# Directed layers: a fused subtract-and-maximum for the low half of the left values, and one-tensor forms for denominator and epsilon

## The chip, the cores and the metric

The kernel runs on one core of one Trainium2 chip. A core has TensorE (PE, with its weight loads, PEld), VectorE (DVE), ScalarE (ACT), GpSimd (POOL) and SyncE (SP, which issues the transfers). Each engine runs its own queue of instructions in order; engines are tied together by semaphores alone. The metric is the device time of one execution in microseconds.

## The reference, cut to what matters

There are 64 graphs of 128 nodes with 384 features, and four layers, each of the form x = x + layer(relu(layernorm(x)), adj). Layers 0 and 3 are attention layers. Layer 1 is a directed layer, and layer 2 is two such layers one behind the other. The changed code computes the directed ones:

```python
u = einsum('bld,bmd->blm', h, h) / sqrt(d)
p = softmax(u, axis=-1)
delta = p * adjacency
attn = delta / (sum(delta, axis=2, keepdims=True) + 1e-10)
h_left  = h @ W_left.T + b_left     # likewise h_self, h_right
ctx = einsum(where(j > i, attn, 0), h_left) + diag_a * h_self + einsum(where(j < i, attn, 0), h_right)
o = (ctx - mean) / sqrt(var + 1e-12) * gamma + beta
return relu(o)
```

The kernel does not divide by the row sum. It carries the context unnormalised and adds 1e-12 times the square of the (scaled) denominator to the variance, which gives the same `o`. That is what `den`, `scaled_den` and `eps` are for.

## The kernel before

All matrix products are done in float16 with every operand split into a high and a low half (`hi` = the value rounded to float16, `lo` = the value minus `hi`), three products for each (`three_products`, lines 138 to 141: L139, L140 and L141 in the profile).

`directed` (from line 916) runs once for L1, with 64 tasks, one for each graph, and once for L2, with 128 tasks, two for each graph ("first" and "second"). In L2 first and second tasks of neighbouring graphs alternate. Each engine has a function `step`, called once per task, that lists its work for this task and for the neighbours: `n_.has(0)` is the task itself, `-1` and `-2` are earlier tasks whose tail is done here, `1` and `2` later ones.

One task: `turn_h` transposes h, `turned_hi` (ScalarE) and `turned_lo` (VectorE, L1137, tile `L_hT_lo`) split it. `similarity` gives u, from which `row_max` (L1142) and the exponent are made. `mask` (L1150) multiplies with the adjacency and sums into `tsum`; `diagonal` (L1155) picks the diagonal. Both are `tensor_tensor_reduce`, which the profile shows as CUSTOM_DVE_ANT_0 followed by DVE_READ_ACCUMULATOR2_ANT. `biased` (L1190) makes `left` and `right` from PSUM. `context_var_eps` (L1211, L1212) serves the task before. `denominator` (L1162), `part_sides` (L1180) and `scaled_denominator` (L1168) follow, then `right`, `left_lo` (L1185), `scaled_eps` (L1173), the addition to x of the task two before (`add_to_x`, L1217, only where that one is not a "first"), statistics of the graph two ahead (`stats`, L1123, only in half of L2's tasks) and `turned_lo` of the next task. ScalarE makes the high halves: left (L1065), sides (`sides_hi`, L1069), then `norm_ctx` (L1081, tile `L_o`), then right (L1065). GpSimd does `ctx_norm` (L993, L995), `sides_lo` (L999), `right_lo` (L1004), `gain` (L1009), `offset` (L1019) and, for a graph two ahead, `norm` (L985, L987).

TensorE, per task: similarity, the left and right projections, the transpose for the next task, the self projection, then the six context matmuls: three for left (needs `left_lo`, `sides_lo`), two with the right values' high half (L1325, L1326), and L1328, which waits for `right_lo`. Next comes the similarity of the next task, which waits for `turned_lo`.

The order of VectorE's queue inside one task is written out by hand:

```python
denominator(n_)
part_sides(n_)
scaled_denominator(n_)
biased(n_, d["r_psum"], d["r_sum"], d["r_lo"], right, r_bank, tables[n_.kind()][3])
left_lo(n_)
scaled_eps(n_)
```

Of the kernel before, what the change touches and what calls it, by code (L numbers as in the profile page):

```python
# [23 lines left out]
ALU = mybir.AluOpType  # L24
# [4 lines left out]
P = 128  # L29
# [7 lines left out]
EPS_LN = 1e-12  # L37
MASKED = -9e15
LOWEST = -3.4e38
LIFT = 2.0 ** 12  # L40
# [89 lines left out]
def wait(eng, sem, value):  # L130

    if isinstance(value, int) and value <= 0:
        return
    eng.wait_ge(sem, value)
# [9 lines left out]
def build(nc, ins, out):  # L144
    with ExitStack() as ctx:
        def sb(stack, name, shape, dt=F32):
            return stack.enter_context(nc.sbuf_tensor(name, shape, dt))
# [756 lines left out]
        d = {}  # L904
# [8 lines left out]
        def directed(tag, phase, graph_base, weights, extras, bias_rows, tables, next_weights):  # L913
# [5 lines left out]
            with ExitStack() as s:  # L919
# [3 lines left out]
                leftv = [sb(s, f"{tag}_left_{a}", [P, D], F16) for a in ("hi", "lo")]  # L923
                rightv = [sb(s, f"{tag}_right_{a}", [P, D], F16) for a in ("hi", "lo")]
                left = sb(s, f"{tag}_left", [P, D])
# [20 lines left out]
                nmax = sb(s, f"{tag}_nmax", [P, 1])  # L946
                zsum = sb(s, f"{tag}_zsum", [P, 1])
                tsum = sb(s, f"{tag}_tsum", [P, 1])
                diag = sb(s, f"{tag}_diag", [P, 1])
                den = sb(s, f"{tag}_den", [P, 1])  # L950
                scaled_den = sb(s, f"{tag}_scaled_den", [P, 1])
                eps = sb(s, f"{tag}_eps", [P, 1])
# [10 lines left out]
                with nc.Block() as block:  # L963
# [155 lines left out]
                    def _(dve):  # L1119
# [39 lines left out]


                        def denominator(n_):
                            dve.scalar_tensor_tensor(out=den[:, :], in0=zsum[:, :], scalar=1e-10 * LIFT, in1=tsum[:, :],  # L1162
                                                     op0=ALU.mult, op1=ALU.add).then_inc(d["den_ready"], 1)

                        def scaled_denominator(n_):
                            wait(dve, d["den_ready"], n_.done())
# [3 lines left out]

                        def scaled_eps(n_):
                            wait(dve, d["scaled_den_ready"], n_.done())
                            dve.scalar_tensor_tensor(out=eps[:, :], in0=scaled_den[:, :], scalar=EPS_LN, in1=scaled_den[:, :],  # L1173
                                                     op0=ALU.mult, op1=ALU.mult).then_inc(d["eps_ready"], 1)

                        def part_sides(n_):

# [4 lines left out]

                        def left_lo(n_):
                            wait(dve, d["l_hi"], n_.done())
                            dve.tensor_tensor(leftv[1][:, :], left[:, :], leftv[0][:, :], ALU.subtract).then_inc(d["l_lo"], 1)  # L1185

                        def biased(n_, psum_sem, sum_sem, lo_sem, full, bank, bias):
                            wait(dve, psum_sem, n_.done())
# [31 lines left out]
                        def step(n_):  # L1220
# [27 lines left out]
                            if n_.has(0):  # L1248
# [6 lines that stand above are left out]
# [114 lines left out]
        for tag, phase, base, weights, next_weights, kinds in (  # L1369
                ("L1", Phase(0, first=4, last=6, after=2), 0, W1, W2, ("only",)),  # L1370
                ("L2", TwoLayerPhase(G, first=3, last=3, after=2), G, W2, W3, ("first", "second"))):
            with ExitStack() as s:
                w_hi, w_lo = (sb(s, f"{tag}_w_{a}", [P, 3 * len(kinds), C, D], F16) for a in ("hi", "lo"))
                bias_rows = sb(s, f"{tag}_bias_rows", [P, len(kinds), D], F16)
                kept_rows = sb(s, f"{tag}_gain_offset_biases", [P, len(kinds), 4, D])

                rows_of = [(n, [5 * n + 1], n) for n in range(len(kinds))]

                def bias_rows_high(act, weights=weights, rows=bias_rows, rows_of=rows_of):
                    weights.bias_rows_high(act, rows, rows_of)  # L1380

                def bias_rows_low(dve, weights=weights, rows=bias_rows, rows_of=rows_of):
                    weights.bias_rows_low(dve, rows, rows_of)

                def keep_rows(pool, weights=weights, number=len(kinds), kept=kept_rows):

                    pool.wait_ge(w_scaled, weights.n_prepared + 1)
                    for n in range(number):
                        pool.tensor_copy(kept[:, n, 0:2], raw_bias[:, 5 * n + 3:5 * n + 5]).then_inc(w_kept_by_pool, 1)
                        for m, b in ((2, 0), (3, 2)):  # L1390
                            pool.tensor_scalar(kept[:, n, m], raw_bias[:, 5 * n + b], scale[:, n:n + 1], None,
                                               ALU.mult).then_inc(w_kept_by_pool, 1)

                weights.begin(w_hi, w_lo, len(kinds), 3 * len(kinds))
                extras = {"act": bias_rows_high, "dve_before": bias_rows_low, "pool": keep_rows}
                directed(tag, phase, base, weights, extras, bias_rows,
                         {kind: [kept_rows[:, n, m] for m in range(4)] for n, kind in enumerate(kinds)}, next_weights)
# [63 lines left out]
```

## Time and profile before

| | |
|---|---|
| median of 3 runs | 2719.62 us (2717.78 to 2720.9) |
| profiled execution | 2719.79 us, span 2718.1 us, mean granted clock 0.981 |
| TensorE busy | 2501.8 us (92%) |
| VectorE busy | 2323.3 us (85%) |
| ScalarE busy | 1815.9 us (67%) |
| GpSimd busy | 1439.5 us (53%) |
| `L_left_lo` (L1185), 192 times | 173.4 us, mean 903 ns |
| `L_den` (L1162), 192 times | 28.4 us, mean 148 ns |
| `L_eps` (L1173), 192 times | 38.9 us, mean 203 ns |

In the profile, a row of the timeline gives the start in us from the span's start, the duration in us, engine, line, operation, tile written and tiles read with their shapes, and in brackets the idle time before it with what ended it. L1 runs from about 655 to 1103 us, L2 from about 1155 to 2005 us. The durations of neighbouring instructions of one engine overlap a little, since the next one starts before the last has drained: what an instruction costs its queue is the distance from its start to the next one's start.

### The profile page before, as it was taken

The page shows a single profiled execution, that of the slowest core. Times are in us where ns is not written, and L with a number is a line of the kernel's source. Part 1 is how long each engine was busy: PE and PEld are TensorE (multiplying, and loading weights), DVE is VectorE, ACT ScalarE, POOL GpSimd, SP SyncE. Part 2 cuts the span into 40 slices and gives each one's busy share as a digit, 9 for nine tenths or more (in the row PEclk, how much of TensorE's full clock was granted, in tenths as well). Part 3 has the DMA queues.
Part 4 walks back from the last instruction along what each step waited for, and adds up shares of the span by engine and source line. Part 5 has one row for each costly group of instructions (what it writes and reads, how often), then busy time and mean ns, then how long its engine had stood idle before and what let it go on. Part 6 is the DMA issues. An engine that isn't in the chain of part 4 may idle for free. (4 is left out here: it accounts for less than half of the span.)

```text
span 2718.1 us, 80319 instructions
## 1 busy us (share of the span) xinstructions
PE 2501.8 (92%) x27969; PEld 1884.9 (69%) x27969; DVE 2323.3 (85%) x9515; ACT 1815.9 (67%) x4409; POOL 1439.5 (53%) x2016
## 2 busy tenths in 40 slices
PE   5999999986999999599999999999969999999998
PEld 4888888884666665466666666666648888888886
DVE  5787878776999999688888888888869999999997
ACT  5888888874556555455566566655638777777775
POOL 2232323223777777467777777777734444444443
PEclk9999999997999999899999999999979999999999
DMA  3111111102000000100000000000000000000000
GB/s 106 29 34 30 33 30 34 29 19 88 10 11 11 11 10 11 45 11 11 11 12 11 11 11 12 11 11 11 12 6 23 28 27 26 29 26 29 26 30 24
DMA packets 74340, 64.67 MB, mean 24 GB/s; under 512 B 7888, under 2 KB 73936, under 8 KB 73936
## 3 DMA queue, kind: packets, MB, share of 16 engines
q1 hardware_dynamic: 73936, 59.54, 7.2%
q8 instruction: 223, 3.65, 0.6%
q14 instruction: 181, 1.48, 0.2%
HBM read 46.92 MB, written 12.58 MB: 22 GB/s over the span
## 5 line engine op out<-in xcount | busy, mean ns | idle before, releaser
L139 PE MATMUL bank<-L_w_hi,L_hT_hi 128*128 128x384 f16 x2112 | 692.3, 328 | 0.0
L140 PE MATMUL bank<-L_w_lo,L_hT_hi 128*128 128x384 f16 x2112 | 692.1, 328 | 0.0
L141 PE MATMUL bank<-L_w_hi,L_hT_lo 128*128 128x384 f16 x2112 | 691.5, 327 | 0.0
L540 ACT ACTIVATE raw_weights<-L_minus_scores,L_minus_max 128x128 f32<-128x128 f32 x1536 | 474.8, 389 | 69.7 <-DVE L_minus_max L655 69.7
L139 PE MATMUL bank<-L_hT_hi,L_w_hi 128*128 128x128 f16 x2304 | 412.6, 220 | 1.3 <-issue 0.8
L140 PE MATMUL bank<-L_hT_lo,L_w_hi 128*128 128x128 f16 x2304 | 412.6, 220 | 0.0
L141 PE MATMUL bank<-L_hT_hi,L_w_lo 128*128 128x128 f16 x2304 | 412.3, 220 | 0.0
L655 DVE CUSTOM_DVE_ANT_0 L_minus_scores<-bank,L_minus_score_bias 128x128 f32<-128x128 f32 x1536 | 348.7, 285 | 10.6 <-issue 6.4
L682 DVE TENSOR_TENSOR L_pT_lo<-bank,L_pT_hi 128x512 f16<-128x512 f32 x384 | 241.1, 683 | 118.4 <-ACT L_pT_hi L562 118.3
L141 PEld LDWEIGHTS bank<-L_w_hi,L_hT_lo 128*128 128x128 f16 x2112 | 207.4, 98 | 138.2 <-issue 2.6
L1059 ACT ACTIVATE L_e<-bank,L_nmax 128x128 f32<-128x128 f32 x192 | 70.5, 367 | 342.6 <-DVE L_nmax L1144 342.6
L473 POOL TENSOR_TENSOR L_ln_scale_bias<-L_var_eps,minus_half 128x1 f32<-128x1 f32 x128 | 70.2, 549 | 402.1 <-DVE L_var_eps L621 401.1
L140 PEld LDWEIGHTS bank<-L_w_lo,L_hT_hi 128*128 128x128 f16 x2112 | 207.4, 98 | 108.5 <-issue 2.0
L139 PEld LDWEIGHTS bank<-L_w_hi,L_hT_hi 128*128 128x128 f16 x2112 | 208.0, 99 | 98.8 <-issue 2.0
L481 POOL TENSOR_TENSOR L_xsum<-L_attended,L_bias_v 128x384 f32<-128x384 f32 x64 | 64.1, 1001 | 383.7 <-DVE L_attended L703 383.7
L1004 POOL TENSOR_TENSOR L_right_lo<-L_right,L_right_hi 128x384 f16<-128x384 f32 x192 | 212.2, 1105 | 89.9 <-ACT L_right_hi L1065 87.2
L562 ACT ACTIVATE L_pT_hi<-bank 128x512 f16<-128x512 f32 x384 | 200.6, 596 | 45.4 <-PE bank L831 45.4
L139 PEld LDWEIGHTS bank<-L_hT_hi,L_w_hi 128*128 128x128 f16 x2304 | 226.7, 98 | 2.3 <-issue 2.2
L140 PEld LDWEIGHTS bank<-L_hT_lo,L_w_hi 128*128 128x128 f16 x2304 | 226.8, 98 | 0.7
L141 PEld LDWEIGHTS bank<-L_hT_hi,L_w_lo 128*128 128x128 f16 x2304 | 226.8, 98 | 0.0
L993 POOL TENSOR_TENSOR L_cln_scale_bias<-L_cvar_eps,minus_half 128x1 f32<-128x1 f32 x192 | 105.7, 550 | 219.1 <-DVE L_cvar_eps L1212 219.1
L1019 POOL TENSOR_TENSOR L_ob<-L_og,L_gain_offset_biases 128x384 f32<-128x384 f32 x192 | 191.3, 997 | 15.1
(165 smaller groups left out, 7514.4 us busy)
## 6 DMA issues: line engine op xcount, KB each, us to landing
adj_tile<-in_adj SPq DMA_DIRECT2D x320, 64.0 KB, 1.8
x<-in_x SPq DMA_DIRECT2D x64, 192.0 KB, 2.5
out<-L_result SPq DMA_DIRECT2D x64, 192.0 KB, 1.9
raw_weights<-in_L_gnn_Wq SPq DMA_DIRECT2D x2, 576.0 KB, 4.1
raw_weights<-in_L_gnn_Wk SPq DMA_DIRECT2D x2, 576.0 KB, 5.5
raw_weights<-in_L_gnn_Wv SPq DMA_DIRECT2D x2, 576.0 KB, 5.2
raw_weights<-in_L_gnn_Wl SPq DMA_DIRECT2D x2, 576.0 KB, 5.9
raw_weights<-in_L_gnn_Ws SPq DMA_DIRECT2D x2, 576.0 KB, 5.5
```

The costliest lines, as they stand in the source:

```text
L139: pe.matmul(out, stat[0], move[0], start=first, stop=False)
L140: pe.matmul(out, stat[0], move[1], start=False, stop=False)
L141: return pe.matmul(out, stat[1], move[0], start=False, stop=last)
L473: pool.tensor_tensor(ln[:, 0:1], ve[:, 0:1], minus_half[:, :], ALU.pow).then_inc(rstd_ready, 1)
L540: last = act.activation(probs[:, n_.slot(k), i, :], scores[:, i, :], ACT.Exp, bias=nmax[:, n_.slot(k), i:i + 1], scale=-1.0)
L562: act.activation(pT[0][:, HC * c:HC * c + HC, :], pT_banks[c][:, :].rearrange("p (h q) -> p h q", h=HC), ACT.Copy).then_inc(pT_hi[c], 1)
L655: last = dve.tensor_tensor_reduce(scores[:, i, :], s_banks[j][:, c128(c)], bias[:, n_.slot(), :], 1.0, -LOWEST, ALU.add, ALU.min, nmax[:, ...
L682: dve.tensor_tensor(pT[1][:, hs, :], pT_banks[c][:, :].rearrange("p (h q) -> p h q", h=HC), pT[0][:, hs, :], ALU.subtract).then_inc(pT_lo[ ...
L993: pool.tensor_tensor(cln[:, 0:1], cve[:, 0:1], minus_half[:, :], ALU.pow).then_inc(d["crstd_ready"], 1)
L1004: pool.tensor_tensor(rightv[1][:, :], right[:, :], rightv[0][:, :], ALU.subtract).then_inc(d["r_lo"], 1)
L1019: pool.tensor_tensor(ob[:, :], og[:, :], tables[n_.kind(k)][1], ALU.add).then_inc(d["tail_ready"], 1)
L1059: act.activation(e[:, :], u_bank[:, 0:P], ACT.Exp, bias=nmax[:, 0:1], scale=scalev, accum_out=zsum[:, :]).then_inc(d["p_ready"], 1)
```

## The change

`left_lo` becomes a `tensor_tensor_reduce`: it writes the same difference and also reduces it by maximum into a new column `lmax`, which nothing reads. `denominator` and `scaled_eps` were `scalar_tensor_tensor` with two tensors of one column and a constant; they become `tensor_scalar` with one tensor of one column, a constant, and the other column as per-partition scalar operand. Values and order of all queues stay.

```diff
+                lmax = sb(s, f"{tag}_left_low_max", [P, 1])
...
                         def denominator(n_):
-                            dve.scalar_tensor_tensor(out=den[:, :], in0=zsum[:, :], scalar=1e-10 * LIFT, in1=tsum[:, :],
-                                                     op0=ALU.mult, op1=ALU.add).then_inc(d["den_ready"], 1)
+                            dve.tensor_scalar(den[:, :], zsum[:, :], 1e-10 * LIFT, tsum[:, 0:1], ALU.mult,
+                                              ALU.add).then_inc(d["den_ready"], 1)
...
                         def scaled_eps(n_):
                             wait(dve, d["scaled_den_ready"], n_.done())
-                            dve.scalar_tensor_tensor(out=eps[:, :], in0=scaled_den[:, :], scalar=EPS_LN, in1=scaled_den[:, :],
-                                                     op0=ALU.mult, op1=ALU.mult).then_inc(d["eps_ready"], 1)
+                            dve.tensor_scalar(eps[:, :], scaled_den[:, :], EPS_LN, scaled_den[:, 0:1], ALU.mult,
+                                              ALU.mult).then_inc(d["eps_ready"], 1)
...
                         def left_lo(n_):
                             wait(dve, d["l_hi"], n_.done())
-                            dve.tensor_tensor(leftv[1][:, :], left[:, :], leftv[0][:, :], ALU.subtract).then_inc(d["l_lo"], 1)
+                            dve.tensor_tensor_reduce(leftv[1][:, :], left[:, :], leftv[0][:, :], 1.0, LOWEST, ALU.subtract, ALU.max,
+                                                     lmax[:, :]).then_inc(d["l_lo"], 1)
```

## Rows read from the trace of the kernel before

**Rows 1.** Windows: stretch (us), length, busy us (instructions) of PE, PEld, DVE, ACT, POOL, PEclk, DMA
```profile
690.00:1060.00 370.00, 362.66 (x2504) 225.90 (x2502) 342.79 (x1280) 217.93 (x479) 281.42 (x427) 1.00 0.04 11
1250.00:1950.00 700.00, 694.88 (x4964) 447.62 (x4963) 611.92 (x2273) 419.50 (x950) 508.11 (x738) 1.00 0.04 11
```
**Rows 2.** Waits in L1, 690 to 1060 us: who waited for whom, us, times, longest
```profile
PEld bank L1328 <- POOL L_right_lo L1004: 22.7, 53, 0.6
PEld bank L139 <- DVE L_hT_lo L1137: 17.8, 53, 0.7
```
**Rows 3.** Timeline, TensorE, L1: last context matmul and first of the next similarity
```profile
834.78 0.34 PE L1328 MATMUL bank<-L_right_lo,L_sides_hi 128*128 128x384 f16 x1
835.21 0.23 PE L139 MATMUL bank<-L_hT_hi 128*128 128x128 f16 x1
```
**Rows 4.** Timeline, VectorE, the same L1 task and the next
```profile
832.50 0.91 DVE L1185 TENSOR_TENSOR L_left_lo<-L_left,L_left_hi 128x384 f16<-128x384 f32 x1
833.34 0.15 DVE L1173 SCALAR_TENSOR_TENSOR L_eps<-L_scaled_den 128x1 f32<-128x1 f32 x1
833.41 0.55 DVE L1217 SCALAR_TENSOR_TENSOR x<-L_ob,x 128x384 f32<-128x384 f32 x1
...
834.62 0.52 DVE L1137 TENSOR_TENSOR L_hT_lo<-bank,L_hT_hi 128x384 f16<-128x384 f32 x1
...
835.92 0.29 DVE L1142 TENSOR_REDUCE L_nraw<-bank 128x1 f32<-128x128 f32 x1
```
**Rows 5.** Timeline, GpSimd, the same L1 task
```profile
832.33 0.67 POOL L999 TENSOR_TENSOR L_sides_lo<-L_sides,L_sides_hi 128x256 f16<-128x256 f32 x1
833.53 1.20 POOL L1004 TENSOR_TENSOR L_right_lo<-L_right,L_right_hi 128x384 f16<-128x384 f32 x1 [0.53 <-ACT L_right_hi L1065]
```
**Rows 6.** Timeline, L1: GpSimd's L987 and VectorE's custom instruction of `diagonal`
```profile
844.28 0.19 POOL L987 TENSOR_TENSOR L_ln_scale_bias<-L_var_eps,L_ln_scale_bias 128x1 f32<-128x1 f32 x1
844.30 0.31 DVE L1155 CUSTOM_DVE_ANT_0 L_junk<-L_e_masked,identity 128x128 f32<-128x128 f32 x1
844.54 0.08 DVE L1155 DVE_READ_ACCUMULATOR2_ANT L_diag<- 128x1 f32 x1
```
**Rows 7.** Timeline, VectorE, L1: small instructions in a row
```profile
838.08 0.20 DVE L1211 TENSOR_SCALAR L_cvar_eps<-L_cmean_var,L_eps 128x1 f32<-128x1 f32 x1
838.20 0.14 DVE L1212 TENSOR_SCALAR L_cvar_eps<-L_cmean_var 128x1 f32<-128x1 f32 x1
838.26 0.14 DVE L1162 SCALAR_TENSOR_TENSOR L_den<-L_zsum,L_tsum 128x1 f32<-128x1 f32 x1
838.32 0.41 DVE L1180 TENSOR_TENSOR L_sides<-bank,ight_of_left_of_diagonal 128x256 f32<-128x256 f32 x1
```
**Rows 8.** Timeline: `sides_hi` in L1; `part_sides` and `sides_hi` in an L2 task with x
```profile
838.77 0.42 ACT L1069 ACTIVATE L_sides_hi<-L_sides 128x256 f16<-128x256 f32 x1
...
1412.66 0.42 DVE L1180 TENSOR_TENSOR L_sides<-bank,ight_of_left_of_diagonal 128x256 f32<-128x256 f32 x1
1413.17 0.40 ACT L1069 ACTIVATE L_sides_hi<-L_sides 128x256 f16<-128x256 f32 x1
```
**Rows 9.** Timeline, L2 task with an x: addition to x and `right_lo`
```profile
1414.73 0.55 DVE L1217 SCALAR_TENSOR_TENSOR x<-L_ob,x 128x384 f32<-128x384 f32 x1
1414.80 1.25 POOL L1004 TENSOR_TENSOR L_right_lo<-L_right,L_right_hi 128x384 f16<-128x384 f32 x1 [0.48 <-ACT L_right_hi L1065]
```
**Rows 10.** Timeline, L2 task without an x: L1328, next similarity, row maximum
```profile
1422.58 0.33 PE L1328 MATMUL bank<-L_right_lo,L_sides_hi 128*128 128x384 f16 x1
1422.78 0.23 PE L139 MATMUL bank<-L_hT_hi 128*128 128x128 f16 x1
1423.51 0.28 DVE L1142 TENSOR_REDUCE L_nraw<-bank 128x1 f32<-128x128 f32 x1
```
**Rows 11.** Timeline, L1: `left_lo` and `sides_lo` starting together
```profile
915.82 0.55 DVE L1185 TENSOR_TENSOR L_left_lo<-L_left,L_left_hi 128x384 f16<-128x384 f32 x1
915.82 1.08 POOL L999 TENSOR_TENSOR L_sides_lo<-L_sides,L_sides_hi 128x256 f16<-128x256 f32 x1 [0.20 <-ACT L_sides_hi L1069]
```

## Prediction

> **What bounds the kernel now.** I read the page first: TensorE is the busiest engine, VectorE the second, and only the two directed stretches hold the changed lines. The windows of the two directed stretches come next [rows 1]: TensorE is busy 362.66 of 370 us in the first (layer L1) and 694.88 of 700 in the second (L2), always at a granted clock of 1.00, its 2.4 GHz level. So little is left to take from it, but whatever delays it is paid. The waits say where it still stops in L1 [rows 2]: 53 times for GpSimd's `right_lo`, 53 times for VectorE's `turned_lo` (tile `L_hT_lo`). A wait that comes 53 times in 370 us means one task in about 7.0 us. The timelines of one task show both. `right_lo` ends at 833.53 + 1.20 = 834.73 and the last context matmul follows at 834.78 [rows 3, 5]; `L_hT_lo` ends at 834.62 + 0.52 = 835.14 and the next similarity starts at 835.21 [rows 3, 4].
>
> Both stops hang on one thing: the two-input reads of VectorE and GpSimd keep each other out. `left_lo` takes 0.91 us for 384 elements, and ends (833.41) 0.41 after `sides_lo` ends (833.00) [rows 4, 5]: it waited for GpSimd, then streamed. Where it starts together with `sides_lo`, it takes 0.55 and `sides_lo` 1.08 instead [rows 11]. One sits still until the other is done, and at a tie VectorE goes first. Then the race repeats: the addition to x starts at 833.41, `right_lo` at 833.53, 0.12 later, loses, and takes 1.20 [rows 4, 5]. Of that 0.29 is blocked time (x streams to 833.41 + 0.41), so 0.91 is its own.
>
> **`left_lo` as tensor_tensor_reduce.** The question is whether the new form keeps clear of GpSimd. The trace answers with the custom instruction of `diagonal`, which has two SBUF inputs too. GpSimd's little L987 starts at 844.28 for 0.19; the custom instruction starts at 844.30 and ends at 844.61, 0.14 after L987's end [rows 6]. 0.14 is the time of 128 elements at the rate at which `left_lo` does 384 in 0.41, so it was released and then streamed, as `left_lo` does. It holds and is held like the old form. The fused form removes no wait, then: it starts at the same place, is released by the same `sides_lo`, and streams at one element at the same rate. What it adds is a read of the accumulator: this starts 0.07 before the custom instruction's end and lasts 0.08 [rows 6], hence between nothing and 0.08. I take nothing, since the read begins where the next instruction of the old form begins, 0.07 before the end [rows 4, 6], and lies almost wholly under the instruction itself. Nobody reads the maximum.
>
> The Trainium skill (Vector Engine (DVE) Microarchitecture Reference, Points that are easy to get wrong) says that a two-input instruction with an accumulator runs at half rate when both sources are SBUF and not bf16. The trace speaks against it: 128 elements in 0.31 including the 0.17 that it stood behind L987. By the page 384 elements would cost some 0.40 more per task; that is a rival below.
>
> **`denominator` and `scaled_eps`.** Both change from two tensors and a constant to one tensor, a constant and a per-partition column. The old form lets the next instruction start after 0.06 to 0.07 (`denominator` 838.26, `part_sides` 838.32; `scaled_eps` 833.34, x 833.41) [rows 4, 7]. The form with a column takes 0.20, and the next instruction starts 0.12 after it (L1211 to L1212), against 0.06 for L1212 without one [rows 7]. So +0.06 for `denominator` and +0.05 for `scaled_eps`; the bounds are 0 (all hidden) and those. `scaled_eps` also stops contending with GpSimd, worth nothing where `left_lo` ends after `sides_lo`.
>
> Where they lie in L1: `denominator` stands ahead of `part_sides`. ScalarE's `sides_hi` starts at 838.77, 0.04 after `part_sides` ends (838.32 + 0.41) [rows 7, 8], so it moves by 0.06, and `sides_lo` and the release of `left_lo` with it. `right_lo` does not move: it follows ScalarE's `norm_ctx` and `right_hi`, which hang on `context_var_eps` ahead of `denominator`. `scaled_eps` is directly between `left_lo` and x. Together the addition to x starts 0.11 later; `right_lo`, blocked until x has streamed, ends 0.11 later; the statistics and `L_hT_lo` are in the same queue behind x and end 0.11 later too. Both stops of TensorE grow together. The next row maximum follows the similarity's start by 0.71 (835.21 to 835.92) [rows 3, 4], and from it the whole next task hangs, so the period grows by the full 0.11. 62 of 64 tasks carry an x: 62 x 0.11 = 6.8 us.
>
> In L2 tasks alternate. In those with an x (A), `sides_hi` starts at 1413.17, 0.09 after `part_sides` ended (1412.66 + 0.42), not 0.04 [rows 8]: ScalarE was busy with the left half. This cover of 0.05 hides `denominator`; without it A would pay 0.06 more. `scaled_eps` is paid: x and with it the blocked `right_lo` (1.25, started 0.07 after x) [rows 9] end 0.05 later, and TensorE waits for that. In those without an x (B) TensorE waits only for `L_hT_lo`: similarity starts 0.20 after the last context matmul (1422.58 to 1422.78), and the row maximum 0.93 after it, now set by the context's addition [rows 10]. I take `sides_hi` there as uncovered, as in L1. `L_hT_lo` then comes 0.11 later, similarity at 0.31, the row maximum at 0.31 + 0.71 = 1.02 instead of 0.93: +0.09. 62 pairs x (0.05 + 0.09) = 8.7 us.
>
> Sum: 6.8 + 8.7 = 15.5 us on the profiled run's 2719.8 (span 2718.1), which is 0.2 above the median: **2735 us**.
>
> **Rivals.** *The race for the port is lost* (slower still). x now starts only 0.01 ahead of `right_lo` in L1 (0.12 - 0.11) and 0.02 in A (0.07 - 0.05) [rows 4, 5, 9]. At a tie VectorE won [rows 11]; 0.02 behind, in `diagonal`, it lost [rows 6]. If x is behind by that, `right_lo` runs its 0.91 alone, to 1.20 + 0.91 = 2.11 after `sides_lo`'s old start, x streams after it and ends at 2.11 + 0.41 = 2.52 instead of 1.63 (833.41 + 0.55 - 832.33). `L_hT_lo` and the period grow by 0.89 in place of 0.11: 62 x 0.89 = 55 us. In A the bounds are 0 and 0.89; `L_hT_lo` is not what TensorE waits for there, so it has slack first, and I take 0.4: 25 us, with B's 5.6. All lost: about 2805. Only A's lost: 6.8 + 25 + 5.6, about 2757.
>
> *The fused instruction does not hold the port* (faster). For it speaks only that rows 6 show small sizes; against it that its end follows L987's end. Then it takes 0.55, x starts 0.61 after `left_lo`'s start (833.11, not 833.41), `right_lo` runs unblocked, and L1 gains 0.30 a task, 19 us. In A at most the blocked 0.34 goes; with 0.28, 17 us. About 2684 us. It decides from the point where `left_lo` is no longer released by `sides_lo`.
>
> *Nothing is seen*: the column forms hidden behind semaphores, as `right` and the matmuls have their own release: 2720.
>
> *Half rate of the fused instruction*: 0.40 on 186 tasks at least, 74 us: 2794, and the race would be lost as well.
>
> **How the numbers follow.** The forecast gets 0.68, with 2726 (only `scaled_eps` paid) to 2746 (the accumulator's read paid in part) as its own range. The lost race gets 0.14, half of it in a part of the tasks only; nothing seen 0.11; the free port 0.05; half rate 0.02. The range 2721 to 2765 takes in the forecast, half of "nothing seen" and the race lost in A alone or now and then. A measurement of this kernel can tell about 0.2% (5.4 us) from no change. Slower by more than that: 0.68 + 0.14 + 0.02 = 0.84; within 0.11; faster 0.05.
>
> **What would show it.** `left_lo`'s fused instruction still at 0.9 to 0.97 us; `denominator` and `scaled_eps` at 0.20; x at 0.55 and starting just before `right_lo`, which takes about 1.31 in L1 and 1.30 in A; L1's period up by 0.11; TensorE's waits for both larger. x at over 1 us and `right_lo` at 0.91 is the lost race. `left_lo` at 0.55 beside a `sides_lo` of 0.67 is the free port. The step I trust least is the 0.01 to 0.02 that is left of the lead.

## The result and the profile after

| | before | changed |
|---|---|---|
| median | 2720.26 us (4 runs) | 2736.26 us (4 runs, 2734.47 to 2739.69) |
| ratio | | 1.0062, 95% interval 1.0044 to 1.0079 |
| span of the profiled execution | 2718.1 us | 2736.3 us |
| L1, second task to last / L2, third task to last | 435.5 / 836.5 us | 440.7 / 846.3 us |
| median period, L1 task / L2 pair | 6.931 / 13.231 us | 7.037 / 13.397 us |

On another chip, with five runs, the changed kernel took 2737.77 us (ratio 1.0066, 1.0053 to 1.0078). The periods here and below are distances from one `right_lo` matmul of TensorE to the next, in the trace.

The three changed instructions in the changed kernel (engine, line, operation, tile, count: shortest/median/longest in ns). One line was added far above, so they stand one line lower.

```profile
L1186 DVE CUSTOM_DVE_ANT_0 L_left_lo<-L_left,L_left_hi x192: 545/958/1060, 660.4 to 2015.3; 128x384 f16<-128x384 f32 x192
L1186 DVE DVE_READ_ACCUMULATOR2_ANT L_left_low_max<- x192: 75/77/86, 661.0 to 2016.2; 128x1 f32 x192
L1163 DVE TENSOR_SCALAR L_den<-L_zsum,L_tsum x192: 196/204/206, 658.2 to 2014.1; 128x1 f32<-128x1 f32 x192
L1174 DVE TENSOR_SCALAR L_eps<-L_scaled_den x192: 202/203/211, 661.0 to 2016.2; 128x1 f32<-128x1 f32 x192
```

`left_lo` is as long as before (it was 547/961/1067), the other two are at 0.20, as a column form was said to be. A steady task of L1, VectorE first, then GpSimd, then TensorE:

```profile
829.06 0.96 DVE L1186 CUSTOM_DVE_ANT_0 L_left_lo<-L_left,L_left_hi 128x384 f16<-128x384 f32 x1
829.96 0.08 DVE L1186 DVE_READ_ACCUMULATOR2_ANT L_left_low_max<- 128x1 f32 x1
829.96 0.20 DVE L1174 TENSOR_SCALAR L_eps<-L_scaled_den 128x1 f32<-128x1 f32 x1
830.08 0.54 DVE L1219 SCALAR_TENSOR_TENSOR x<-L_ob,x 128x384 f32<-128x384 f32 x1
...
831.30 0.53 DVE L1138 TENSOR_TENSOR L_hT_lo<-bank,L_hT_hi 128x384 f16<-128x384 f32 x1
...
828.94 0.67 POOL L1000 TENSOR_TENSOR L_sides_lo<-L_sides,L_sides_hi 128x256 f16<-128x256 f32 x1
830.09 1.31 POOL L1005 TENSOR_TENSOR L_right_lo<-L_right,L_right_hi 128x384 f16<-128x384 f32 x1 [0.47 <-ACT L_right_hi L1066]
...
831.45 0.34 PE L1330 MATMUL bank<-L_right_lo,L_sides_hi 128*128 128x384 f16 x1
831.88 0.23 PE L139 MATMUL bank<-L_hT_hi 128*128 128x128 f16 x1
```

Set beside [rows 4, 5]: `left_lo` is released by `sides_lo` (828.94 + 0.67 = 829.61) and ends 0.41 after it, as before. x starts at 830.08, only 0.01 ahead of `right_lo` at 830.09; it was 0.12. x keeps the port (0.54), and `right_lo` is held off longer: 1.31 where it took 1.20.

In 19 tasks of the changed kernel, however, x does not take 0.55. There `left_lo` comes first and `sides_lo` is the one that is held:

```profile
878.42 0.55 DVE L1186 CUSTOM_DVE_ANT_0 L_left_lo<-L_left,L_left_hi 128x384 f16<-128x384 f32 x1
879.02 0.90 DVE L1219 SCALAR_TENSOR_TENSOR x<-L_ob,x 128x384 f32<-128x384 f32 x1
...
878.44 1.06 POOL L1000 TENSOR_TENSOR L_sides_lo<-L_sides,L_sides_hi 128x256 f16<-128x256 f32 x1
```

x now waits behind `sides_lo`. In the kernel before, `scaled_eps` stood in that wait (over 0.4 us in 22 tasks, up to 661 ns) and x took 0.55 behind it. The new form of `scaled_eps` only hands the wait on to x.

The windows of the same stretches (columns as in [rows 1]) and TensorE's waits, first those of L1, then those of L2:

```profile
690.00:1060.00 370.00, 358.25 (x2474) 223.19 (x2473) 346.01 (x1318) 214.95 (x473) 283.09 (x421) 1.00 0.04 11
1250.00:1950.00 700.00, 692.50 (x4910) 442.08 (x4908) 619.93 (x2343) 415.72 (x939) 511.53 (x731) 1.00 0.04 11
...
PEld bank L1330 <- POOL L_right_lo L1005: 27.4, 53, 0.5
PEld bank L139 <- DVE L_hT_lo L1138: 17.5, 53, 0.3
...
PEld bank L1330 <- POOL L_right_lo L1005: 37.8, 105, 0.6
PEld bank L139 <- DVE L_hT_lo L1138: 12.5, 47, 0.6
```

TensorE is busy 358.25 of 370 us in L1 (362.66 before) and 692.50 of 700 in L2 (694.88). In L1 the wait for `right_lo` grew (22.7 before); the one for `turned_lo` did not (17.8 before, 17.5 now). In L2 the wait for `right_lo` went from 35.2 to 37.8, and one for `turned_lo`, 1.0 in 2 times before, is there 47 times.

### The profile page after: what moved, and what is told of

The parts are those of the page before. It is cut to its first block and busy times, and to the rows that moved or that the text cites. A ratio compares the mean times of both kernels' runs of the same rounds, so it can differ in the third digit from the quotient of the medians.

```text
span 2736.3 us, 80511 instructions
## 1 busy us (share of the span) xinstructions
PE 2509.0 (92%) x27969; PEld 1885.1 (69%) x27969; DVE 2350.8 (86%) x9707; ACT 1816.4 (66%) x4409; POOL 1453.9 (53%) x2016
## 5 line engine op out<-in xcount | busy, mean ns | idle before, releaser
L1005 POOL TENSOR_TENSOR L_right_lo<-L_right,L_right_hi 128x384 f16<-128x384 f32 x192 | 220.4, 1148 | 81.5 <-ACT L_right_hi L1066 79.5
```

Source lines behind the costliest of these rows:

```text
L1005: pool.tensor_tensor(rightv[1][:, :], right[:, :], rightv[0][:, :], ALU.subtract).then_inc(d["r_lo"], 1)
```

## The experiments

### One part of the change at a time

`fused_only`: the kernel before with `left_lo` alone as in the change.

> Kernel before with only left_lo as tensor_tensor_reduce. Theory (each edit costs what it adds to the start-to-start distance ahead of the addition to x): the trace of the changed kernel has scaled_eps 0.346 us after the end of sides_lo where it was 0.336, so 0.01 per task, 62 x 0.01 in L1 and about as much in each L2 pair: +1 to +2 us, 2721 to 2723; left_lo stays at 0.91 to 0.97 us where sides_lo releases it. Rival (the fused form and its accumulator read carry the loss): +10 to +17 us, 2730 to 2737, and the distance from left_lo to scaled_eps grows by 0.05 or more.

`den_only`: the kernel before with `denominator` alone as in the change.

> Kernel before with only denominator as tensor_scalar with a column. Theory: 0.06 ahead of part_sides moves sides_hi, sides_lo and the release of left_lo by 0.055 in L1 (62 x 0.055 = 3.4 us) and in L2's tasks without an x, where similarity starts 0.26 instead of 0.20 after the last context matmul and the row maximum 0.97 instead of 0.94 (62 x 0.03 = 1.9 us); nothing in L2's tasks with an x (ScalarE's 0.05 of cover). About +5 us, 2725. Rival (hidden behind the semaphores of right): +0, 2720.

`eps_only`: the kernel before with `scaled_eps` alone as in the change.

> Kernel before with only scaled_eps as tensor_scalar with a column. Theory: distance to the addition to x 0.126 instead of 0.07, +0.056 in L1 (3.5 us), in L2's tasks with an x (3.5 us) and +0.03 in those without (1.9 us): +9 us, 2729. The lead of x over right_lo shrinks from 0.12 to 0.065 in L1 and from 0.073 to 0.02 in L2, and x still wins. Rival (only the fused form counts): +0 to +2 us.

`delay_only`: no form changed, one small instruction added.

```diff
+                spare = sb(s, f"{tag}_spare", [P, 1])
...
                                 scaled_eps(n_)
+                                dve.tensor_scalar(spare[:, :], scaled_den[:, :], 1.0, None, ALU.mult)
                             if n_.has(-2) and n_.kind(-2) != "first":
                                 add_to_x(n_, -2)
```

> Kernel before with one more small tensor_scalar (128x1, a constant, result unused) between scaled_eps and the addition to x. No operand form changes. Theory (what counts is the delay of x, not the form of the instruction): 0.06 more ahead of x, as eps_only: +9 to +10 us, 2729 to 2730. Rival (the forms themselves cost, through the port or the column operand): +0 to +3 us here while eps_only has more.

All four shared a chip; the kernel before took 2717.76 us there.

| | median us | ratio (95% interval) | L1 period | L2 pair |
|---|---|---|---|---|
| before | 2717.76 | | 6.931 | 13.231 |
| fused_only | 2725.24 | 1.0024 (1.0015 to 1.0033) | 6.945 | 13.240 |
| den_only | 2724.57 | 1.0024 (1.0015 to 1.0032) | 6.984 | 13.268 |
| eps_only | 2729.05 | 1.0035 (1.0023 to 1.0048) | 6.983 | 13.316 |
| delay_only | 2733.46 | 1.0052 (1.0039 to 1.0064) | 6.993 | 13.335 |

The periods moved as the distances said: `denominator` +0.053 in L1 and +0.037 a pair (0.055 and 0.03 expected), `scaled_eps` +0.052 and +0.085 (0.056 and 0.086), the fused form +0.014 and +0.009. An instruction that has nothing to do with forms or the port, but stands ahead of x, costs at least as much as the new form of `scaled_eps`: +0.062 and +0.104. So it is the delay of x, and of `turned_lo` behind it, that counts, not what causes it. Which of the two delays weighs how much these runs do not separate. The rival that the fused form carries the loss falls on the periods.

The medians of `fused_only` and `delay_only`, however, are several us above what their periods give. `fused_only` should have been 1 to 2 us slower and was 6 to 7 by its ratio; `delay_only` should have been 9 to 10 slower and was 14 by its ratio. Both have 192 more instructions, and that was tried by itself.

`padded`: the kernel before with one more small instruction where VectorE waits anyway.

```diff
+                spare = sb(s, f"{tag}_spare", [P, 1])
...
                                 scaled_denominator(n_)
+                                dve.tensor_scalar(spare[:, :], tsum[:, :], 1.0, None, ALU.mult)
                                 biased(n_, d["r_psum"], ...)
```

> The kernel before with one more small tensor_scalar (128x1, a constant, result unused) per task where VectorE waits for the right projection anyway, between scaled_denominator and right: 192 more instructions, as fused_only and the changed kernel have, and nothing moved (0.06 of 0.17 to 0.3 us idle). Theory of a cost of the added instructions outside the steady tasks: +3 to +5 us, as what is left of fused_only's +6.5 beyond its steady 1.5, with the end after the last directed task at 719 to 722 us instead of 717.7. Rival (that rest belongs to the fused form itself or to scatter): within 2 us of the kernel before.

It took 2723.87 us beside 2719.34, ratio 1.0018 (1.0009 to 1.0027), with the periods of the kernel before (6.930 and 13.233). The 192 instructions cost 2 to 7 us though the median periods are the same. Most of it lies where no line differs: in the profiled execution the stretch behind the last directed task takes 721.5 us instead of 717.7. Compared there instruction by instruction, the 3.8 us come in three parts.

First, 1.5 us are lost within the first 45 us. As much is lost in `eps_only` and `x_behind` as well, which have no more instructions than the kernel before, and not in `fused_only`, so this part does not go with the added instructions. What makes it stays open.

Second, 1.0 us is lost in four steps, 136, 188, 240 and 292 us behind the last task. At the first, one instruction of VectorE starts late while it waits for nothing that the profile shows (kernel before, then `padded`):

```profile
2134.45 0.23 DVE L694 SCALAR_TENSOR_TENSOR L_rnorm<-L_rsum,weight_unscale,L_keep 128x12 f32<-128x12 f32 x1
2138.65 0.23 DVE L694 SCALAR_TENSOR_TENSOR L_rnorm<-L_rsum,weight_unscale,L_keep 128x12 f32<-128x12 f32 x1 [0.44 <-issue]
```

All seven traces of kernels with 192 more instructions show this wait in the same place, with the same 1.0 us. The six with none more do not, and neither does `pushed`, which has 384 more. So this part goes with where in the queue the instructions come to stand, and does not grow with the number added.

Third, 1.3 us are lost in the last 30. The same work is done at a lower mean granted clock of TensorE, 0.75 instead of 0.85 (windows of the kernel before and of `padded`, columns as in [rows 1]):

```profile
2690.40:2718.10 27.70, 16.95 (x165) 10.57 (x161) 16.02 (x53) 10.29 (x29) 4.81 (x4) 0.85 0.07 23
2695.30:2724.30 29.00, 18.47 (x165) 11.60 (x161) 16.16 (x53) 10.46 (x28) 4.80 (x4) 0.75 0.06 21
```

The runs say the same of the whole: the mean granted clock is 0.980 in 9 of 11 executions of `padded` and 0.981 or 0.982 in 14 of 15 of the kernel before. Why the clock fell and why the one instruction is issued late stays open. Nor is it a fixed price: the same stretch took 719.0 and 721.6 us in the two profiles of the changed kernel, 719.9 in `fused_only` and 717.8 in `pushed`. It is of the size of what was left over in `fused_only`, but that run was not taken apart further.

### The whole change again, and x pushed over the edge

`changed_again` is the changed kernel in one call with the next three.

> The changed kernel itself, on the chip and in the call of the next three. Theory (sum of start-to-start distances ahead of the addition to x): +15 to +17 us over the kernel before, 2733 to 2735 beside a 2718; steady period 7.03 to 7.04 in L1, a pair of L2 at 13.40. Rival (a fixed cost of the 192 more instructions outside the steady tasks): +20 us or more.

It took 2737.77 us beside 2719.50, ratio 1.0066 (1.0053 to 1.0078), periods 7.040 and 13.392. The ratio gives 18 us, between the two expectations: about 15 of the directed tasks and a few us outside them.

`pushed`: the changed kernel with the small instruction of `delay_only` added, in the same place.

> The changed kernel with one more small tensor_scalar (128x1, a constant, result unused) between scaled_eps and the addition to x. In the changed kernel x starts only 0.002 to 0.008 us before right_lo and still gets the port. Theory (whoever asks first for the second SBUF input holds the other off for the whole instruction): with 0.06 more x comes 0.06 behind right_lo, loses, stretches from 0.55 to about 1.4 us, right_lo falls from 1.31 to 0.91, and turned_lo behind x comes 0.8 later: L1's period 7.83, 50 us, and 0.3 to 0.4 per L2 pair, 20 us: about 2800 to 2810. Rival (the two share the port or the cost is simply the added distance): as delay_only, +10 to +15 us over the changed kernel, 2745 to 2750.

It took 2792.67 us, ratio 1.0265 (1.0251 to 1.0279): 55 us above the changed kernel for an instruction whose queue distance is 0.06. One task of `pushed`, GpSimd and VectorE:

```profile
835.31 0.91 POOL L1006 TENSOR_TENSOR L_right_lo<-L_right,L_right_hi 128x384 f16<-128x384 f32 x1 [0.48 <-ACT L_right_hi L1067]
836.17 1.31 POOL L1011 TENSOR_TENSOR L_og<-L_o,L_gain_offset_biases 128x384 f32<-128x384 f32 x1
...
835.30 0.14 DVE L1258 TENSOR_SCALAR L_spare<-L_scaled_den 128x1 f32<-128x1 f32 x1
835.36 1.27 DVE L1220 SCALAR_TENSOR_TENSOR x<-L_ob,x 128x384 f32<-128x384 f32 x1
836.55 0.55 DVE L1125 BATCH_NORM_STATS2 L_bn<-x 128x6 f32<-128x384 f32 x1
```

x starts 0.05 behind `right_lo`, stands still until that ends, and takes 1.27; the statistics start 1.19 after it instead of 0.47. `right_lo` is down to 0.91. 106 of 128 additions to x take over 1 us. L1's period is 7.822 (7.83 expected) and the L2 pair 13.734. The total is lower than expected (2800 to 2810): the two stretches together grew by 59 us over the changed kernel's first profile instead of 70, since the last tasks and some in between lost less, and the stretch behind them was 1.2 us shorter.

The changed kernel itself shows one such task, and also how late x may come. In the first pair of lines `right_lo` is first by 0.09 and x loses; in the second, of L2, by 0.01 and x still wins:

```profile
681.59 0.91 POOL L1005 TENSOR_TENSOR L_right_lo<-L_right,L_right_hi 128x384 f16<-128x384 f32 x1 [0.38 <-ACT L_right_hi L1066]
681.68 1.24 DVE L1219 SCALAR_TENSOR_TENSOR x<-L_ob,x 128x384 f32<-128x384 f32 x1
...
1210.06 1.33 POOL L1005 TENSOR_TENSOR L_right_lo<-L_right,L_right_hi 128x384 f16<-128x384 f32 x1 [0.46 <-ACT L_right_hi L1066]
1210.07 0.55 DVE L1219 SCALAR_TENSOR_TENSOR x<-L_ob,x 128x384 f32<-128x384 f32 x1
```

Over all traces the latest x that still won started 0.031 us after `right_lo` (in `delay_only`), the earliest that lost 0.033 us after it (in `fused_only`). For `left_lo` and `sides_lo` the edge lies elsewhere: in the kernel before, `left_lo` lost when it started 0.017 us after `sides_lo`; in `padded` it won at up to 0.039.

### Where x stands in the queue

`x_behind`: no instruction added or removed, x moved behind `turned_lo`.

```diff
-                            if n_.has(-2) and n_.kind(-2) != "first":
+                            add_x = n_.has(-2) and n_.kind(-2) != "first"
+                            add_first = n_.has(1) and n_.kind(1) == "second"
+                            if add_x and add_first:
                                 add_to_x(n_, -2)
...
                                 turned_lo(n_, 1)
+                            if add_x and not add_first:
+                                add_to_x(n_, -2)
```

> The kernel before with the addition to x moved behind turned_lo in VectorE's queue (except where the next task is an L2 'second' one, which needs it earlier). No instruction is added or removed. Theory (x holds right_lo off, and x stands ahead of turned_lo): right_lo takes 0.91 everywhere, turned_lo comes 0.46 earlier, both stops of TensorE go: L1's period 6.93 to about 6.49 (27 us), L2's tasks with an x 6.76 to 6.48 (17 us): about -44 us, 2674. Rival (TensorE is the bound, busy 98 to 99% of both stretches): no more than its idle time there can go, 7 of 370 and 5 of 700 us, at most -15 us, 2703.

`x_behind_changed`: the same move in the changed kernel.

> The changed kernel with the same move of the addition to x. Theory: right_lo no longer depends on VectorE, so what is left of the change's cost is turned_lo, 0.12 later where statistics stand ahead of it (L1 and half of L2), and nothing in L2's tasks with an x: +0.10 per L1 task and +0.11 per L2 pair over x_behind, +11 to +14 us, about 2687. Rival (with the race gone the change is free): as x_behind.

Both expectations failed, in opposite directions: `x_behind` took 2732.00 us (ratio 1.0044, 1.0030 to 1.0058), slower than before, and `x_behind_changed` 2698.84 (0.9925, 0.9912 to 0.9937). In this order the change is worth 33 us. One L1 task of `x_behind`:

```profile
839.60 0.55 DVE L1185 TENSOR_TENSOR L_left_lo<-L_left,L_left_hi 128x384 f16<-128x384 f32 x1
840.07 0.63 DVE L1173 SCALAR_TENSOR_TENSOR L_eps<-L_scaled_den 128x1 f32<-128x1 f32 x1
...
841.81 1.29 DVE L1217 SCALAR_TENSOR_TENSOR x<-L_ob,x 128x384 f32<-128x384 f32 x1
...
839.62 1.05 POOL L999 TENSOR_TENSOR L_sides_lo<-L_sides,L_sides_hi 128x256 f16<-128x256 f32 x1
840.82 0.91 POOL L1004 TENSOR_TENSOR L_right_lo<-L_right,L_right_hi 128x384 f16<-128x384 f32 x1
841.69 0.99 POOL L1009 TENSOR_TENSOR L_og<-L_o,L_gain_offset_biases 128x384 f32<-128x384 f32 x1
```

`right_lo` is at 0.91, as expected, and `turned_lo` comes earlier. But the row maximum then comes earlier too, `left_lo` starts ahead of `sides_lo` and wins, and `scaled_eps`, which in its old form has two SBUF inputs, is the one that is held (0.63 for a column of one element). x arrives 0.12 after `gain` (L1009) has started, is held for 1.29, and the next task's front waits for VectorE: the period is 7.300. (The L2 pair gained, 13.011, but by less than L1 lost.) I had looked at the race with `right_lo` and not at the one with the instruction behind it. The same place in `x_behind_changed`:

```profile
838.22 0.55 DVE L1186 CUSTOM_DVE_ANT_0 L_left_lo<-L_left,L_left_hi 128x384 f16<-128x384 f32 x1
838.69 0.08 DVE L1186 DVE_READ_ACCUMULATOR2_ANT L_left_low_max<- 128x1 f32 x1
838.69 0.21 DVE L1174 TENSOR_SCALAR L_eps<-L_scaled_den 128x1 f32<-128x1 f32 x1
...
840.29 0.55 DVE L1219 SCALAR_TENSOR_TENSOR x<-L_ob,x 128x384 f32<-128x384 f32 x1
...
838.48 0.82 POOL L1000 TENSOR_TENSOR L_sides_lo<-L_sides,L_sides_hi 128x256 f16<-128x256 f32 x1 [0.37 <-ACT L_sides_hi L1070]
...
840.36 1.34 POOL L1010 TENSOR_TENSOR L_og<-L_o,L_gain_offset_biases 128x384 f32<-128x384 f32 x1
```

`scaled_eps` is at 0.21, x starts 0.07 ahead of `gain` and wins: period 6.708. The fused `left_lo`, not held here, takes 0.55, and `scaled_eps` starts 0.47 after it, just as behind the old form in `x_behind`.

`x_behind_eps`: `x_behind` with the new form of `scaled_eps` alone.

> The moved kernel x_behind with one part of the change, scaled_eps as tensor_scalar with a column; left_lo and denominator as before. In x_behind left_lo starts just ahead of sides_lo and wins, scaled_eps (two SBUF inputs) is then held for 0.63 us by sides_lo, turned_lo comes late, and x loses to gain (1.29 us). Theory (the one-tensor form is not held by GpSimd, and that turned x_behind's 2732 into 2699): scaled_eps at 0.20 everywhere, x at 0.55, about 2690 to 2700. Rival (the fused form or the 0.06 of denominator did it): near 2732.

2696.92 us, ratio 0.9917 (0.9904 to 0.9931), L1's period 6.718. The form of `scaled_eps` alone turned 2732 into 2697; the fused form and `denominator` had no measurable part in it (2698.84 with them).

`x_early`: the kernel before with x ahead of `right`, in VectorE's wait for the right projection.

```diff
                                 scaled_denominator(n_)
+                                if n_.has(-2) and n_.kind(-2) != "first":
+                                    add_to_x(n_, -2)
                                 biased(n_, d["r_psum"], d["r_sum"], d["r_lo"], right, r_bank, tables[n_.kind()][3])
...
-                            if n_.has(-2) and n_.kind(-2) != "first":
+                            if not n_.has(0) and n_.has(-2) and n_.kind(-2) != "first":
                                 add_to_x(n_, -2)
```

> The kernel before with the addition to x moved ahead, between scaled_denominator and right, where VectorE stands idle for 0.17 to 0.3 us and GpSimd does only instructions of one column. Nothing is added or removed. Theory (x is then out of all races with right_lo, sides_lo and gain, and right has 0.3 us of room before ScalarE takes it up): x 0.55, right_lo 0.91, L1's period about 6.5 instead of 6.93, L2's tasks with an x about 6.5 instead of 6.76: -40 us, 2678. Rival (x delays right, or holds off L995 and with it norm_ctx, so that the gain is given back): 2700 to 2720.

2688.10 us, ratio 0.9883 (0.9868 to 0.9898): the fastest of all, 1.2% below the kernel before, though 10 us short of the expectation. The periods are 6.574 (6.5 expected) and 13.042. VectorE and GpSimd in one task, and the two windows:

```profile
836.50 0.55 DVE L1217 SCALAR_TENSOR_TENSOR x<-L_ob,x 128x384 f32<-128x384 f32 x1
836.97 0.55 DVE L1190 TENSOR_TENSOR L_right<-bank,L_gain_offset_biases 128x384 f32<-128x384 f32 x1
...
836.77 0.33 POOL L995 TENSOR_TENSOR L_cln_scale_bias<-L_cvar_eps,L_cln_scale_bias 128x1 f32<-128x1 f32 x1
...
690.00:1060.00 370.00, 368.04 (x2621) 235.06 (x2620) 340.44 (x1341) 220.45 (x502) 282.51 (x446) 1.00 0.04 11
1250.00:1950.00 700.00, 699.28 (x5029) 453.27 (x5027) 605.97 (x2295) 425.17 (x961) 500.48 (x748) 1.00 0.04 12
```

No x is held and no `right_lo`. The rival was right in small: x holds off L995 (0.33 instead of 0.19). TensorE is busy 368.04 of 370 us and 699.28 of 700.

`x_early_changed`: the same in the changed kernel.

> The changed kernel with the same early addition to x. Theory: with x out of the way the change costs only what it puts ahead of turned_lo where statistics stand there (0.12 in L1 and in half of L2), +5 to +14 us over x_early. Rival (scaled_eps freed from GpSimd pays here too, as in x_behind_changed): below x_early by 5 us or more.

2704.06 us (0.9943, 0.9931 to 0.9956), 16 us above `x_early`, slightly more than expected; the periods are 6.629 and 13.191. `scaled_eps` freed from GpSimd pays nothing here, since `left_lo` ends after `sides_lo` again. `x_behind_eps`, `x_early` and `x_early_changed` shared a chip with the kernel before at 2719.57, `x_behind` and `x_behind_changed` one with it at 2719.50.

## Why the prediction was right

**What the fused form costs.** The conclusion held: the fused form contends with GpSimd as the old one does, `left_lo` at 545/958/1060 ns against 547/961/1067. But the reading it was drawn from was wrong. The prediction took the 0.31 of `diagonal` [rows 6] for 0.17 of waiting behind L987 and 0.14 of streaming. The line's durations in the kernel before (shortest/median/longest) say otherwise:

```profile
L1155 DVE CUSTOM_DVE_ANT_0 L_junk<-L_e_masked,identity x192: 264/292/308, 655.3 to 1996.3; 128x128 f32<-128x128 f32 x192
```

77 of the 192 have no GpSimd instruction beside them, and those take 0.29 too. The one of [rows 6] was held for 0.02 at most. So those rows could hardly tell the forecast from the free port, and the 0.05 given to that rival had little to rest on; that the fused form waits is shown only by the runs that have it, where it ends 0.41 after `sides_lo` in the task above. The forecast was lucky here. "0.02 behind, in `diagonal`, it lost" falls with the same reading.

Half rate is ruled out: unblocked the fused form takes 0.55, and its successor starts 0.47 after it, as behind the old form. The Trainium skill (Vector Engine (DVE) Microarchitecture Reference, Points that are easy to get wrong) states half the throughput for one instruction layout, `S2S2D2_STT`, with two SBUF sources that are not bf16, for want of a port for the accumulator; this instruction, with one fp32 and one fp16 source and an accumulator, does not show it, and no run shows which layout it has. "Nothing" for the accumulator's read was slightly low: 0.014 a task in L1, 0.009 a pair.

**`denominator` and `scaled_eps`.** Predicted 0.06 and 0.05 of distance, measured by themselves 0.053 and 0.052 in L1's period; the cover of 0.05 under which `denominator` was to disappear in A held, as `den_only` cost 0.037 a pair, close to what B alone gives.

**The sums.** L1 was predicted at 0.11 a task and had 0.106; from the second task to the last this made 5.2 us instead of 6.8: the last five tasks and eight in between grew by 0.04 or less or became shorter, and the one lost race cost about 1. TensorE's two waits were both to grow; in L1 only that for `right_lo` did (22.7 to 27.4 us). `turned_lo` comes later by as much as the matmul ahead of it, so the wait between them stays (17.8 and 17.5). The L2 pair was predicted at 0.14 and has 0.166 by the median: x in A came 0.07 later relative to `right_lo` rather than 0.05 (0.057 for `scaled_eps` and 0.01 for the fused form), which explains 0.02 of the 0.026. That is 9.8 us instead of 8.7. Together 15.0 us, against 15.5.

**What the sum left out.** The profiled executions differ by 18.2 us; about 3 of them lie outside the directed tasks, 1.3 behind the last one, of the kind seen in `padded`. No step spoke of that. The measured +16 to +18 us holds both; that the sum alone came within 2 us of the median is partly luck, because L1's tasks gave back part of what this took.

**The race.** The remaining lead was put at 0.01 and 0.02. By the median it is 0.007 in L1 and 0.003 in A, and in six places x started behind `right_lo` and still won, so the outcome hung on who wins a tie. That VectorE does was read from a single place [rows 11]. `pushed` shows what was at stake, 55 us more, near the 70 that the rival was priced above the forecast. That the change stayed on the near side was therefore partly luck as well: the edge for this pair, 0.03 behind, was not visible before. The Trainium skill (SBUF — State Buffer, Who interferes with whom) says that a VectorE instruction with two SBUF inputs contends with GpSimd's reads, and that issue order decides who blocks. The traces agree with the first, x at 0.55, 0.89 or 1.27. By the start times of the profile they agree with the second but for the last 0.03 us, in which x was later and still won.

**The free port and "nothing is seen"** did not occur: in none of the 192 tasks did `left_lo` and `sides_lo` both run at full speed side by side, and both column forms were paid.

## What to carry to other kernels

Where VectorE and GpSimd both read two tensors from SBUF, look for pairs of instructions that start within a few hundredths of a microsecond of each other, and ask what a shift of 0.1 does to who is first: the loser stands still for the other's whole length, with all that is queued behind it. An instruction moved to a place where the other engine reads nothing large is worth more than a saving in its form (here 31 us for one moved addition, against 17 lost by three new forms). When an order is changed, walk through every instruction of the other engine that the moved one may now meet, not only the one it met before.

## What the runs showed of the hardware that I had not expected

- For x and `right_lo` the tie has a sharp edge. VectorE's addition still got the port when it started up to 0.031 us after GpSimd's `right_lo`, and lost it from 0.033 us on. It is not one number for all pairs: `left_lo` lost to `sides_lo` at 0.017 in the kernel before, and won at up to 0.039 in `padded`.
- A `tensor_scalar` on one element per partition with a column as scalar operand starts its successor 0.126 us later, against 0.07 for the form with two tensors; yet the former is never held by GpSimd (202 to 211 ns over 192 times), and the latter took up to 661 ns.
- 192 small instructions in an idle place of VectorE's queue cost 4.5 us (1.0018, 1.0009 to 1.0027), most of it in a stretch in which they do not stand. The trace shows 1.0 us there in four small steps, the first a wait of 0.44 us for "issue" in one place, and a lower granted clock at the end. With 384 more (`pushed`) neither is there.
